# Half-width value weights with one unit per batch, and output weights' low parts one query head earlier on POOL

## The reference, cut to what matters

```python
q = (query @ Wq).reshape(b, t, h, d)      # query = layernorm(x), 32 heads of 128
k = (key @ Wk).reshape(b, t, kv_h, d)     # key = value = ctx_4096, 8 heads of 128
v = (value @ Wv).reshape(b, t, kv_h, d)
q = apply_rope(q); k = apply_rope(k)
logits = 30.0 * jnp.tanh(einsum(q, k) * 0.08838834764831845 / 30.0)   # then the causal mask
attn = softmax(logits) @ v
return attn @ Wo
```

## Time and profile before

| | us |
|---|---|
| median of 3 runs | 3444.82 |
| lowest, highest | 3442.93, 3447.54 |
| the profiled execution | 3447.87 |
| its span in the trace | 3446.1 |
| first stage, PE's first to last matmul | 10.33 to 370.7 |
| attention stage, first `out` to the last pass | 1365 to 3168 |
| PE busy | 3139.9 |

### The profile page before, as it was taken

How to read it: one execution, slowest core, us unless ns; L and a number is a source line. 1 busy time by engine, 2 the same in 40 slices (tenths; PEclk the granted TensorE clock), 3 DMA queues, 4 the chain that set the end, 5 groups by cost and what they waited for, 6 DMA issues and landing times. The chain is left out here.

```text
span 3446.1 us, 42643 instructions
## 1 busy us (share of the span) xinstructions
PE 3139.9 (91%) x15315; PEld 2547.2 (74%) x15315; DVE 2066.1 (60%) x2603; ACT 1235.9 (36%) x1898; POOL 1856.7 (54%) x1247
## 2 busy tenths in 40 slices
PE   8999589999999957999989898889999899998699
PEld 8999467887788745777777777777777777777577
DVE  3222367777777634756556666657575666665575
ACT  3111255555555522333333333333333333332322
POOL 4222454544454435666666666766666766664343
PEclk9999799999999978999999999999999999999799
DMA  7333411111111132222323222332223232221321
GB/s 203 111 123 116 142 37 56 38 55 62 50 44 62 37 118 86 81 102 74 109 103 129 91 91 91 116 134 97 85 97 106 89 133 80 96 87 66 138 80 49
DMA packets 157218, 315.76 MB, mean 92 GB/s; under 512 B 10360, under 2 KB 74488, under 8 KB 157096
## 3 DMA queue, kind: packets, MB, share of 16 engines
q1 hardware_dynamic: 157096, 314.17, 25.8%
HBM read 247.03 MB, written 67.11 MB: 91 GB/s over the span
## 5 line engine op out<-in xcount | busy, mean ns | idle before, releaser
L1896 PE MATMUL gp_y<-g_wo_hi,g_at_hi 128*128 128x512 f32 x992 | 414.4, 418 | 123.9 <-POOL g_wo_lo L1528 122.9
L1782 DVE RECIPROCAL g_rsum<-gp_sum 128x512 f32<-128x512 f32 x128 | 429.1, 3352 | 57.7 <-PE gp_sum L1872 57.7
L1840 PE MATMUL gp_p<-g_xn_hi,g_wq_hi 128*128 128x512 f32 x1024 | 404.5, 395 | 27.9 <-POOL g_wq_lo L1528 27.9
L1896 PE MATMUL gp_y<-g_wo_lo,g_at_hi 128*128 128x512 f32 x992 | 408.0, 411 | 0.0
L1896 PE MATMUL gp_y<-g_wo_hi,g_at_lo 128*128 128x512 f32 x992 | 406.7, 410 | 0.0
L1840 PE MATMUL gp_p<-g_xn_lo,g_wq_hi 128*128 128x512 f32 x1024 | 403.1, 394 | 0.0
L1840 PE MATMUL gp_p<-g_xn_hi,g_wq_lo 128*128 128x512 f32 x1024 | 402.8, 393 | 0.0
L1896 PEld LDWEIGHTS gp_y<-g_wo_hi,g_at_hi 128*128 128x128 f32 x992 | 198.6, 200 | 192.5 <-POOL g_wo_lo L1528 136.0
L1762 DVE SCALAR_TENSOR_TENSOR g_res<-gp_y,g_tg,g_res 128x512 f32<-128x512 f32 x256 | 188.2, 745 | 205.6 <-PE gp_y L1896 185.2
L1528 POOL TENSOR_TENSOR g_wq_lo<-g_wq_raw,g_wq_hi 128x1024 fp32r<-128x1024 f32 x130 | 310.3, 2410 | 1.7 <-ACT g_wq_hi L1626 1.7
L1559 POOL TENSOR_TENSOR g_q_raw<-g_q_raw,g_rot_b 128x512 f32<-128x512 f32 x128 | 227.6, 1778 | 135.5 <-DVE g_rot_b L1745 135.5
(11 more groups left out here) (254 smaller groups left out, 7525.6 us busy)
## 6 DMA issues: line engine op xcount, KB each, us to landing
g_wq_raw<-in_L_Wq SPq DMA_DIRECT2D x64, 1024.0 KB, 7.4
g_wo_raw<-in_L_Wo SPq DMA_DIRECT2D x62, 1024.0 KB, 6.1
values_split<-c_v SPq DMA_DIRECT2D x64, 256.0 KB, 2.6
keys_split<-c_k SPq DMA_DIRECT2D x32, 512.0 KB, 2.6
g_k<-keys_split SPq DMA_DIRECT2D x32, 512.0 KB, 3.2
g_v<-values_split SPq DMA_DIRECT2D x32, 512.0 KB, 7.6
c_cx_raw<-in_ctxT SPq DMA_DIRECT2D x16, 512.0 KB, 7.3
a_x<-in_x SPq DMA_DIRECT2D x16, 512.0 KB, 4.5
```

Source lines behind the costliest of these rows:

```text
L1782: V.reciprocal(rsum[:, :], p_sum[:, :]).then_inc(rsum_done, 1)
L1840: mm = M(bank[:, :], w[a][:, i, cols], x[b][:, i, :], start=(i == 0 and t == 0), stop=(i == KT - 1 and t == 2))
L1896: mm = M(p_y[u % 2][:, :], at[p][:, h, bcols(b)], w[r][:, h, half_ * BANK:(half_ + 1) * BANK], start=(h == 0 and t == 0), stop=(h == G - 1 ...
```

## The change

It has two parts.

**The first stage.** A value unit is now one batch times 512 columns of `Wv` (four heads): 8 x 3 matmuls of 512 columns. There are still 32 value units, four in each round, but rounds 0 to 3 use the first half of `Wv` and rounds 4 to 7 the second. A half is 2 MB and comes in four DMAs (`piece`), whose low parts POOL (0 and 2) and DVE (1 and 3) make. Batches 4 to 15 are now rounded by ACT three at a time, behind each of the first four `v_round`; DVE makes the low part of batch 4 + i behind `v_low(0, i)`. The store of a unit writes runs of 128 columns (512 B) where it wrote 256.

**The attention stage.** POOL makes the low part of `Wo`'s head 0 behind `rotated(n + 1, 0)` and that of head 1 behind `rotated(n + 1, 1)`, each one head earlier.

```diff
@@ key_value_stage @@
-    VW = 2
+    VW = 4
-    PAIRS = BATCH // 2
-    PER_J = PAIRS // VW
+    PER_J = BATCH * NKV // VW // NKV
+    PIECES = 4
...
             def load_wv(q):
                 if q > 0:
-                    sp.wait_ge(made, made_v(2 * q - 1, PER_J - 1))
+                    sp.wait_ge(made, made_v(q * NKV // 2 - 1, PER_J - 1))
                 src = Wv.rearrange("(k p) (q n) -> q p k n", p=P, n=VC)[q]
-                for i in range(2):
-                    sp.dma_start(khalf(i)(wv["raw"]), khalf(i)(src)).then_inc(wv_land[i], 16)
+                for i in range(PIECES):
+                    sp.dma_start(piece(i)(wv["raw"]), piece(i)(src)).then_inc(wv_land[i], 16)
...
                 sp.wait_ge(emptied, made_v(j, i))
-                for w in range(VW):
-                    sp.dma_start(v_out[g * NKV + VW * quarter(j) + w][:, :, h * 2 * HD:(h + 1) * 2 * HD],
-                                 v_sb[n % 2][:, :, w, :].bitcast(F32)).then_inc(v_store[n % 2], 16)
+                for m in range(2):
+                    sp.dma_start(v_out[first:first + VW].rearrange("w p s n -> p w s n")[:, :, m, cols],
+                                 v_sb[n % 2][:, m, :].bitcast(F32).rearrange("p (w n) -> p w n", w=VW))\
+                        .then_inc(v_store[n % 2], 16)
...
@@ scalar @@
             wk_round(0)
-            for b in range(4, 6):
-                cx_round(b)
             for j in range(NKV):
                 for i in range(PER_J):
                     v_round(j, i)
                     if j == 0:
-                        for b in range((6, 9, 12, 14)[i], (9, 12, 14, 16)[i]):
+                        for b in range(3 * i + 4, 3 * i + 7):
                             cx_round(b)
...
@@ vector @@
-            for b in range(4):
+            cx_low(0)
+            wv_low(0)
+            for b in range(1, 4):
                 cx_low(b)
             for j in range(NKV):
                 for i in range(PER_J):
-                    if j == 0 and i < 2:
-                        cx_low(2 * i + 4)
-                        cx_low(2 * i + 5)
                     v_low(j, i)
+                    if j == 0:
+                        cx_low(4 + i)
                     if i == 1:
                         wk_low(j)
                 for g in range(NGRP):
                     rotate(j, g)
+                    if g == 0 and j == NKV // 2 - 1:
+                        wv_low(1)
...
@@ tensor @@
-                for m in range(2):
-                    b = 2 * pair(j, i) + m
-                    if q == 0:
-                        cx_ready(b)
-                    for k in range(KT):
-                        if pair(j, i) == 0 and m == 0 and k % (KT // 2) == 0:
-                            pe.wait_ge(wv_lo, wv_count(q, 2 * k // KT))
-                        for t, (x, w) in enumerate(SPLIT):
-                            mm = M(out[:, m, :, :], tokens(b)(cx[x])[:, k, :], by_head(wv[w][:, k, :]),
-                                   start=(k == 0 and t == 0), stop=(k == KT - 1 and t == 2))
+                if q == 0:
+                    cx_ready(b)
+                for k in range(KT):
+                    m, rest = divmod(k, KT // PIECES)
+                    if b == 0 and rest == 0:
+                        pe.wait_ge(wv_lo_dve if m % 2 else wv_lo_pool, PIECES // 2 * q + m // 2 + 1)
+                    for t, (x, w) in enumerate(SPLIT):
+                        mm = M(bank(u)[:, :], tokens(b)(cx[x])[:, k, :], wv[w][:, k, :],
+                               start=(k == 0 and t == 0), stop=(k == KT - 1 and t == 2))
                 mm.then_inc(made, 1)
...
@@ gqa_stage, gpsimd @@
                     for i in range(NR):
                         rotated(n + 1, i)
-                        if 1 <= i < 3:
-                            wo_split(n, i - 1, wo)
+                        if i < 2:
+                            wo_split(n, i, wo)
```

More of the change, by code:

```diff
@@ L73, in key_value_stage @@
         k_sb = [sb(f"k{i}", [P, 2, BANK], F32R) for i in range(2)]
-        v_sb = [sb(f"v{i}", [P, 2, VW, 2 * HD], F32R) for i in range(2)]
+        v_sb = [sb(f"v{i}", [P, 2, VC], F32R) for i in range(2)]
         rot = [sb(f"rot{i}", [P, BANK]) for i in range(2)]
@@ L79, in key_value_stage @@
         cx_land = [sem(f"cx_land{i}") for i in range(BATCH)]
-        wv_land = [sem(f"wv_land{i}") for i in range(2)]
+        wv_land = [sem(f"wv_land{i}") for i in range(PIECES)]
         wk_land, table_in = sem("wk_land"), sem("table_in")
         cx_hi, cx_lo_dve, cx_lo_pool = sem("cx_hi"), sem("cx_lo_dve"), sem("cx_lo_pool")
-        wk_hi, wk_lo, wv_hi, wv_lo = sem("wk_hi"), sem("wk_lo"), sem("wv_hi"), sem("wv_lo")
+        wk_hi, wk_lo, wv_hi = sem("wk_hi"), sem("wk_lo"), sem("wv_hi")
+        wv_lo_dve, wv_lo_pool = sem("wv_lo_dve"), sem("wv_lo_pool")
         made, emptied = sem("made"), sem("emptied")
@@ L101, in k_count, with half, batch @@
             return j * NGRP + g + 1
-        def quarter(j):
-            return j * PER_J // PAIRS
-        def pair(j, i):
-            return (j * PER_J + i) % PAIRS
+        def half(j):
+            return j * PER_J // BATCH
+        def batch(j, i):
+            return (j * PER_J + i) % BATCH
         def bank(u):
             return p_u[(u - 1) % NPS]
-        def by_head(t):
-            return t.rearrange("p (w n) -> p w n", w=VW)
         def after(engine, done, count):
@@ L169, in _ @@
                     store_v(j, i)
-                if j % 2 == 1 and j + 1 < NKV:
-                    load_wv(quarter(j + 1))
+                if j == NKV // 2 - 1:
+                    load_wv(1)
                 for g in range(NGRP):
@@ L177, in _ @@
                 sp.wait_ge(k_store[i], 16 * NKV * NGRP // 2)
[L178 to L181 removed]
+                sp.wait_ge(v_store[i], 32 * NKV * PER_J // 2)
         @block.scalar
@@ L194, in wv_round @@
             def wv_round(q):
-                for i in range(2):
+                for i in range(PIECES):
                     act.wait_ge(wv_land[i], 16 * (q + 1))
-                    round_hi(wv, khalf(i)).then_inc(wv_hi, 1)
+                    round_hi(wv, piece(i)).then_inc(wv_hi, 1)
             def wk_round(j):
@@ L205, in v_round @@
                 act.wait_ge(made, made_v(j, i))
-                after(act, v_store[n % 2], 16 * VW * ((n - 1) // 2))
-                A(v_sb[n % 2][:, 0, :, :], by_head(bank(made_v(j, i))[:, :]), ACT.Copy).then_inc(v_hi, 1)
+                after(act, v_store[n % 2], 32 * ((n - 1) // 2))
+                A(v_sb[n % 2][:, 0, :], bank(made_v(j, i))[:, :], ACT.Copy).then_inc(v_hi, 1)
             def k_round(j, g):
@@ L230, in _ @@
                     k_round(j, g)
-                    if g == 0 and j % 2 == 1 and j + 1 < NKV:
-                        wv_round(quarter(j + 1))
+                    if g == 0 and j == NKV // 2 - 1:
+                        wv_round(1)
         @block.vector
@@ L244, in wk_low, with wv_low @@
                 low(V, wk, lambda t: t[:, :, :]).then_inc(wk_lo, 1)
+            def wv_low(q):
+                for i in range(1, PIECES, 2):
+                    dve.wait_ge(wv_hi, PIECES * q + i + 1)
+                    low(V, wv, piece(i)).then_inc(wv_lo_dve, 1)
             def v_low(j, i):
-                n = v_count(j, i)
-                dve.wait_ge(v_hi, n)
-                t = v_sb[n % 2]
-                V.tensor_tensor(t[:, 1, :, :], by_head(bank(made_v(j, i))[:, :]), t[:, 0, :, :].bitcast(F32),
-                                ALU.subtract).then_inc(emptied, 1)
+                dve.wait_ge(v_hi, v_count(j, i))
+                t = v_sb[v_count(j, i) % 2]
+                V.tensor_tensor(t[:, 1, :], bank(made_v(j, i))[:, :], t[:, 0, :].bitcast(F32), ALU.subtract)\
+                    .then_inc(emptied, 1)
             def rotate(j, g):
@@ L290, in wv_low @@
             def wv_low(q):
-                for i in range(2):
-                    pool.wait_ge(wv_hi, wv_count(q, i))
-                    low(G, wv, khalf(i)).then_inc(wv_lo, 1)
+                for i in range(0, PIECES, 2):
+                    pool.wait_ge(wv_hi, PIECES * q + i + 1)
+                    low(G, wv, piece(i)).then_inc(wv_lo_pool, 1)
             def cx_low(b):
@@ L313, in _ @@
                     finish_k(j, g)
-                    if g == 0 and j % 2 == 1 and j + 1 < NKV:
-                        wv_low(quarter(j + 1))
+                    if g == 0 and j == NKV // 2 - 1:
+                        wv_low(1)
         @block.tensor
```

14 lines of the change are left out of this document (6 added, 8 removed).

## The result

| | before | after |
|---|---|---|
| median of 4 runs each, us | 3446.18 | 3302.02 |
| lowest, highest | 3442.93, 3449.43 | 3298.29, 3307.61 |
| the profiled execution | 3447.87 | 3307.61 |
| its span | 3446.1 | 3305.8 |

The ratio is 0.9583, with a 95% interval of 0.9565 to 0.9601: the change takes 144 us away. The forecast was 3294 us, and the time lies inside 3260 to 3328, 8 us above the forecast.

The account below looks back on a forecast made before the run. PE bounds the kernel, busy 3139.9 of 3446.1 us, so gains come from its idle time, slow clock or matmul count. 3447.87 less 152 plus 1.3 is 3297.2; with the median 3.05 lower, 3294 us, range 3260 to 3328.

Parts of the forecast that it names:

- The wait for the low part of `Wo`: Attention loop: PE's 31 waits for POOL's low part, 122.9 us in all, go, with 2.1 us to spare.
- What is late next: Attention loop: blocked POOL adds delay the queries' low parts, so PE waits 1.0 us before `scores` instead of 4.0.
- 4.9 us a pass, 152 in all: Attention loop: `scores` comes 4.9 us earlier in each of 31 passes, 152 us in all.
- handed on whole: Attention loop behind `scores`: engine lists are unchanged, so the whole 4.9 us shift carries through each pass.
- The first stage, the matmuls: First stage: 512-column value matmuls save 8.6 us over 28 units and 1.2 us in the first four.
- The first stage, the wait: First stage, before `key(0, 1)`: PE stands 9.4 us for batch 7's low part, plus 1.7 slow clock: +11.1 us.
- (a): Attention loop: the wait is gone whole and PE is the bound; 3264 us, chance 0.12.
- (b): First stage: it gains its 10 us too, as the store lands earlier or units fall better; 3283 us, chance 0.10.
- (c): Attention loop: the 1.0 us wait keeps the clock low, +53 us; 3347 us, chance 0.06.
- (d): Behind `scores`: another wait, for the probabilities' or `Wq`'s low parts, keeps a third of the gain; 3345 us, chance 0.07.
- (e): Attention loop: slower than before, as POOL stands for a late `Wo` with later rotations queued; 3539 us, chance 0.02.
- (f): First stage: a 512-column value matmul costs as much as two of 256; 3304 us, chance 0.05.

Follow-up runs that it names:

- the first experiment: The attention stage's part of the change alone, on the kernel before: 3298.26 us, ratio 0.9576.
- the repair on DVE: The kernel after, with DVE making both of its low parts of `Wo` (heads 2 and 3) behind rotation 1: 3282.44 us, ratio 0.9525.
- the shorter wait in the loop: The kernel after, with POOL making `Wo` head 0 one rotation earlier but head 1 where it was, behind rotation 2: 3407.96 us, ratio 0.9895.
- the second experiment: The first stage's part of the change alone, the kernel after with POOL's `Wo` lines turned back: 3446.12 us, ratio 1.0001.

## Why the prediction was right, point by point

**The wait for the low part of `Wo`.** Right, shown: it is gone in all 31 passes, and the first experiment gives the whole gain with those lines alone.

**What is late next.** Right in mechanism and place. Laid over the pass at 1962.27 (all times 49.91 earlier than in the pass of the earlier trace rows), the chain that was worked out holds to 0.2 us at each step: the add of rotation 1 at 1954.2 for 2.33 and measured 1954.15 for 2.27, the add of rotation 2 at 1960.9 for 2.27 and 1960.76 for 2.28, rotation 3 at 1963.2 and 1963.14, POOL's last subtraction ending at 1968.7 and 1968.6. That the two adds would be blocked again was the choice on which 4.9 stood and not 5.86. The kernel without DVE's part of head 3 shows the blocking to be the cause, and by the 0.66 us that came for 1.0 it also shows that the bound below, 5.86 a pass with PE as the limit, couldn't be had: the chain behind the last projection is 0.5 us longer than `out`. The rule of the Trainium skill (SBUF — State Buffer, "SBUF: two separate sides"), by which one of the two holds the ports for a whole instruction, agrees with the trace: 1.29 or 2.28 us for the same add, and nothing between. DVE's parts do take lengths between (1.22, 1.5 and 2.4 to 2.7 us): in the rows above, those of 1.54 and 2.73 us both end 1.1 us behind the POOL operation that they met. What the prediction drew from the rule, that POOL's quarter right ahead of DVE's makes DVE's part block the next add, is what the repair on DVE gave 20 us for.

**4.9 us a pass, 152 in all.** The first `out` to `scores` gained 149.9 us over the 31 passes (353.3 to 203.4), and behind `scores` each pass lost 0.1 again, some 3 in all; the whole stage gained 146.9. The term was 5 us too large: 2 in the chain, and 3 in "handed on whole". The row at 1968.85 has it: the matmul behind the wait is followed 0.33 us later, where 0.23 is the rule, and by the time of the pass's first projection `scores` has lost 0.1 us, in the kernel after and in the first experiment alike.

**The first stage, the matmuls.** -8.6 was worked out for the 28 units and -9.1 measured (313.7 to 304.6). The rows of before had the right price, and the formula of the Trainium skill (TensorE: Matmul & The Clock Gate, "Back-to-back issue gap"), by which it would have been -1.8, doesn't hold here: 0.227 us for 512 columns stands against its 0.216. That section gives the formula for an isolated matmul, and says itself that it misses a stream in which each matmul loads its weights; the prediction left that out. The first four units were to take 23.5 and took 24.75, since the slow clock at the start lasted until 16.98, 3.0 us and not 1.7. That is the spread of executions: with the same front the other kernels' profiles have it end between 13.2 and 16.2, and the four units take 23.2 to 24.3. So 23.5 was a fair size for the term and the profiled execution an unlucky one. PE's start at 10.88 instead of 10.33 was left out of the sum; the kernels with this front start at 10.5 to 10.9 and those with the old one at 10.3.

**The first stage, the wait.** The right wait at the right place, for batch 7's low from DVE, to 48.4 where 48.7 was forecast, and the store landed at 42.5 as worked out. It lasted 7.2 us and not 9.4, since PE came 1.9 us later. The slow clock behind it cost 2.95 and not 1.7 (three key units in 19.30 us, and 3 x 5.45 is 16.35): the loop's price was carried to another place, and it differs from wait to wait, as the shorter wait in the loop showed. PE's late coming and the shorter wait offset each other by the mechanism, since DVE's list sets when the wait ends, whenever PE comes. The slow clock's error stays: in all round 1 begins 10.9 us late, against a forecast of 9.9. That the stage ended at +1.8, so near the +1.3, is in part luck, since the matmuls behind it brought 0.5 more than forecast. That it nets to nothing is measured by the second experiment. POOL's last low came at 59.9 (60.7 forecast) and PE passed it unhindered.

**The rivals.** (a), the wait gone whole, is refuted with its mechanism, since the floor is 5.92 and not 5.45. (b), the first stage gains too, is refuted for this change and true of another order of the lists: the kernel with ACT's and DVE's order changed has them, 9.0 us by the end of its first stage. (c), a wait of 1.0 us that keeps the clock low, is refuted by the clock of 1.00 in the pass and 0.99 over the loop. The kernel with the shorter wait shows that it was worth its chance: behind 2.8 us the clock falls in 26 of 31 passes of the profiled execution. (d) and (e) did not happen; `g_prob_lo` took 14.7 us before and 14.6 after, and `Wo` had a median of 6.4 us to landing, never waited for by ACT. (f) is refuted: 56 units in 304.64 us are 5.44 each, or 0.227 a matmul, value units and key units alike.

**What is left between forecast and result.** The sum gave 3297.2 for the profiled execution, which took 3307.6. Of the 10.4 us the attention stage has 5.1, the first stage 0.5, and the stages that the change doesn't touch 4.8. The median lies 5.6 below this execution, and 3.05 were assumed, so 8 us remain.
